# Second cross-attention of a perceiver block: probabilities turned in 32x32 blocks on VectorE, weighted means in four row tiles of TensorE, key rows fetched ready from DRAM

## The reference

```python
xn = layer_norm(x, g_media, b_media)          # x: context, 64 x 257 x 128
ln = layer_norm(latents, g_latent, b_latent)  # 64 x 32 x 128
q = (ln @ Wq).reshape(B, Q, 16, 64).transpose(0, 2, 1, 3) * scale
kv = jnp.concatenate([xn, ln], axis=1) @ Wkv
k, v = jnp.split(kv, 2, axis=-1)              # each 16 heads of 64
sim = jnp.einsum('bhqd,bhfd->bhqf', q, k)
sim = jnp.where(full_mask[:, None, None, :], max_neg, sim)   # latents are never masked
alphas = jax.nn.softmax(sim, axis=-1)
out = jnp.einsum('bhqf,bhfv->bhqv', alphas, v)
return out.transpose(0, 2, 1, 3).reshape(B, Q, 1024) @ Wout + bout
```

## Time and profile before

| | us |
|---|---|
| median of 3 runs | 1558.25 |
| lowest and highest of them | 1556.33, 1567.27 |
| the profiled execution, its time | 1562.48 |
| the profiled execution, span from first to last instruction | 1560.7 |
| experts, from the first to the last of their `up` products | 464 to 700 |
| second cross-attention, its scores from first to last | 760.4 to 1307.9 |
| second cross-attention, last product | 1317 |

### The profile page before, as it was taken

The page is one execution under the profiler, slowest core; times in us unless marked ns, Lnnn a source line. Parts: engine busy times, 40 slices in busy tenths (PEclk is TensorE's granted clock), DMA queues, the critical chain, the costliest instruction groups (busy, mean ns, idle before and its releaser), DMA issues. The chain is left out here.

```text
span 1560.7 us, 36610 instructions
## 1 busy us (share of the span) xinstructions
PE 1362.0 (87%) x12406; PEld 1038.3 (67%) x12406; DVE 851.6 (55%) x2728; ACT 804.3 (52%) x1838; POOL 146.0 (9%) x432
## 2 busy tenths in 40 slices
PE   5799999666759999997899999999999999577855
PEld 2677777366536777775688888888888887212433
DVE  3466666478433444444555555555555554654387
ACT  3588888278314444442555555455555554444423
POOL 0122221364001111110000000000000000000000
PEclk8899999899669999997999999999999999787965
DMA  3332331000012111110000000000000000000000
GB/s 96 89 75 73 76 74 50 1 0 0 0 52 86 55 55 47 48 41 0 20 17 16 21 15 19 15 19 15 19 15 19 15 21 4 1 0 1 20 1 27
DMA packets 58225, 47.58 MB, mean 30 GB/s; under 512 B 11048, under 2 KB 55600, under 8 KB 58032
## 3 DMA queue, kind: packets, MB, share of 16 engines
q1 hardware_dynamic: 58160, 46.74, 10.9%
HBM read 36.07 MB, written 1.18 MB: 24 GB/s over the span
## 5 line engine op out<-in xcount | busy, mean ns | idle before, releaser
L1426 ACT ACTIVATE d_p<-bank,d_nmax 128x289 f32<-128x289 f32 x256 | 128.8, 503 | 239.0 <-DVE d_nmax L1472 238.9
L1364 PE MATMUL bank<-d_pT,d_xv 128*128 128x128 f32 x1536 | 220.3, 280 | 0.1
L1472 DVE TENSOR_REDUCE d_nmax<-bank 128x1 f32<-128x289 f32 x256 | 116.7, 456 | 171.3 <-PE bank L1345 169.6
L1364 PEld LDWEIGHTS bank<-d_pT,d_xv 128*128 128x128 f32 x1536 | 191.3, 191 | 12.1 <-ACT d_pT L1418 6.3
L1344 PE MATMUL bank<-d_key,d_q 128*128 128x289 f32 x512 | 167.3, 408 | 0.6 <-ACT d_q L1411 0.4
L1162 ACT ACTIVATE c_hs<-bank,c_w 128x512 f32<-128x512 f32 x128 | 87.8, 687 | 147.1 <-PE bank L1085 145.6
L431 ACT ACTIVATE a_p<-a_p,a_nmax 128x257 f32<-128x257 f32 x256 | 115.5, 500 | 38.6 <-DVE a_nmax L470 38.5
L1353 PE MATMUL bank<-ident,d_p 128*128 128x128 f32 x768 | 125.9, 273 | 0.1
L1418 ACT ACTIVATE d_pT<-bank 128x384 f32<-128x384 f32 x256 | 123.0, 480 | 0.9 <-PE bank L1353 0.8
L1085 PE MATMUL bank<-yT,c_w 128*128 128x512 f32 x256 | 118.2, 606 | 6.0 <-DMA c_w<-in_L_ffn_w 6.0
L1094 PE MATMUL bank<-c_w,c_hs 128*128 128x128 f32 x1024 | 122.0, 278 | 0.0
(11 more groups left out here) (268 smaller groups left out, 2304.6 us busy)
## 6 DMA issues: line engine op xcount, KB each, us to landing
d_key<-x_keyT SPq DMA_DIRECT2D x64, 144.5 KB
a_ctT<-in_ctxT SPq DMA_DIRECT2D x64, 128.5 KB, 2.1
a_low<-mask_low SPq DMA_DIRECT2D x64, 128.5 KB, 3.0
c_ct<-in_ctx SPq DMA_DIRECT2D x64, 128.0 KB, 2.2
c_w<-in_L_ffn_w SPq DMA_DIRECT2D x8, 514.0 KB, 3.8
xT<-in_xT SPq DMA_DIRECT2D x4, 256.0 KB, 3.5
a_vlast<-values_last SPq DMA_DIRECT2D x4, 256.0 KB, 6.4
d_maskb<-mask_bf SPq DMA_DIRECT2D x64, 0.5 KB
```

Source lines behind the costliest of these rows:

```text
L1364: ins = nc.tensor.matmul(OP[:, 128 * g:128 * g + 128], xv[:, b % 2, k, :], pT[:, u % 2, k, :], start=(k == 0), stop=(k == 2))
L1426: nc.scalar.activation(P[:, u % 4, 0:KEYS], S[u % 2], ACT.Exp, bias=nmax[:, u % 4:u % 4 + 1], accum_out=total[:, u % 4:u % 4 + 1]).then_in ...
L1472: nc.vector.tensor_reduce(nmax[:, u % 4:u % 4 + 1], S[u % 2], AXX, ALU.max, negate=True).then_inc(max_made, 1)
```

## The change

1. In the experts, VectorE now applies the whole affine layer norm to the context rows: `normalise` has two passes over the four tiles, `(x - mean) * gamma` and then `* rstd + beta`, each a `scalar_tensor_tensor` with a row of `x_media` (gamma and beta along the free axis, the same in all partitions). A new semaphore `centred` stands between them. `keep` becomes a plain copy, with the keys in another order.
2. SyncE stores each pair's finished rows to a DRAM tensor `key_rows` (64 batches x 32 x 10 x 128): key 8k+r of a batch lies at [k][r], row 8 of each k holds a latent, row 9 the last context row or zeros. The store of a pair is four transfers of 64 KB, issued ahead of the load of a later pair.
3. The mask is stored as float32 `-3.39e38` times the mask, in the new key order, and is fetched for each batch to all 128 partitions (`d_low`).
4. In the cross-attention TensorE no longer adds the mask, transposes the probabilities or makes key rows. Scores read `keyT` directly. The custom instruction adds the mask, writes the scores to SBUF and gives the maximum; ScalarE's exponential runs in place there; GpSimd normalises; VectorE turns the probabilities in 32x32 blocks into `d_pT`. Key k of block r then lies on partition k of each row tile, where row tile j holds head j of each group.
5. `means` is, once for a batch, ten blocks x four row tiles of 32 partitions: 40 products, each 32 keys by 128 columns, tile j into bank 2+j. The key rows come from DRAM, 32 partitions x 5120 bytes repeated four times in one transfer (`d_xr`, two slots).
6. Queries and projection are spread out: four products of each in every batch. ScalarE copies the means out. The final normalisation writes over `yT`.

```diff
@@ class Context
+        self.media, self.blank = sb("x_media", [128, 2, 128]), sb("x_blank", [128, 128])
+        self.low_dram = core.nc.dram_tensor("mask1_low", (BATCH, CTX + LAT), F32, kind="Internal").ap()
+        self.rows_dram = core.nc.dram_tensor("key_rows", (BATCH, 32, 10, 128), F32, kind="Internal").ap()
...
@@ experts_0, sync
+                def store_pair(i, s):
+                    sp.wait_ge(normed, i * UNITS + (s + 2))
+                    for b in range(2):
+                        for k in range(2):
+                            rows = cx.rows_dram[bass.ds(i * (2 * UNITS) + (2 * s + b), 1), 16 * k:16 * k + 16, 0:8, :].rearrange("b k r d -> (b k) r d")
+                            sp.dma_start(rows, ct[:, s % RING, 2 * b + k, :]).then_inc(cx.rows_stored[s % RING], 16)
+
+                def next_pair(i, s):
+
+                    store_pair(i, s - 3)
+                    sp.wait_ge(turned, i * UNITS + (s - RING + 2))
+                    sp.wait_ge(cx.rows_stored[s % RING], (i * 2 + s // RING) * 64)
+                    load_pair(i, s)
...
@@ experts_0, scalar, keep
-                        keys = cx.keyT[:, bass.ds(i * (2 * UNITS) + 2 * s, 2), 0:256]
-                        src = TC[s % 2].rearrange("p (b k) -> p b k", b=2)
-                    nc.scalar.activation(keys, src, ACT.Identity, scale=cx.affine[:, 0:1], bias=cx.affine[:, 1:2]).then_inc(kept, 1)
+                        keys = cx.keyT[:, bass.ds(i * (2 * UNITS) + 2 * s, 2), 0:256].rearrange("p b (r k) -> p b k r", r=8)
+                        src = TC[s % 2].rearrange("p (b k r) -> p b k r", b=2, r=8)
+                    nc.scalar.activation(keys, src, ACT.Copy).then_inc(kept, 1)
...
@@ experts_0, vector, normalise
                     for m in range(tiles):
-                        ins = nc.vector.tensor_scalar(ct[0:rows, at, m, :], ct[0:rows, at, m, :], moments[0:rows, at, m, 0:1],
-                                                      rstd[0:rows, at, m:m + 1], ALU.subtract, ALU.mult)
+                        ins = nc.vector.scalar_tensor_tensor(ct[0:rows, at, m, :], ct[0:rows, at, m, :], moments[0:rows, at, m, 0:1],
+                                                             cx.media[0:rows, 0, :], ALU.subtract, ALU.mult)
+                    ins.then_inc(centred, 1)
+                    dve.wait_ge(centred, i * UNITS + (s + 2))
+                    for m in range(tiles):
+                        ins = nc.vector.scalar_tensor_tensor(ct[0:rows, at, m, :], ct[0:rows, at, m, :], rstd[0:rows, at, m:m + 1],
+                                                             cx.media[0:rows, 1, :], ALU.mult, ALU.add)
                     ins.then_inc(normed, 1)
...
@@ cross_attention_1, sync
+                def rows(i, b, first=False):
+
+                    n = i * EIGHT + b
+                    if not first:
+                        sp.wait_ge(o_made, n - 1)
+                    rows = cx.rows_dram[bass.ds(n, 1)].rearrange("b k r d -> b k (r d)").broadcast_to([4, 32, BLOCKS * 128])
+                    sp.dma_start(xr[:, b % 2].rearrange("p r d -> p (r d)"), rows).then_inc(xr_loaded[b % 2], 16)
...
@@ cross_attention_1, gpsimd
+                def normalise(i, u):
+                    b, g = divmod(u, GROUPS)
+                    pool.wait_ge(recip, i * UNITS + (u + 1))
+                    p = P[:, b % 2, g, 0:KEYS]
+                    nc.gpsimd.tensor_tensor(p, p, rtotal[:, b % 2, g:g + 1].broadcast_to([128, KEYS]), ALU.mult).then_inc(normed, 1)
...
@@ cross_attention_1, tensor
+                def means(i, b, first=False):
+
+                    n = i * EIGHT + b
+                    pe.wait_ge(xr_loaded[b % 2], (i * (EIGHT // 2) + b // 2) * 16 + 16)
+                    pe.wait_ge(turned, (n + 1) * GROUPS)
+                    if not first:
+                        pe.wait_ge(o_copied, n)
+                    for k in range(BLOCKS):
+                        for j in range(4):
+                            rows = slice(32 * j, 32 * j + 32)
+                            ins = nc.tensor.matmul(O[j], xr[rows, b % 2, k, :], pT[rows, b % 2, :, 32 * k:32 * k + 32], start=(k == 0), stop=(k == BLOCKS - 1))
+                    ins.then_inc(o_made, 1)
...
@@ cross_attention_1, vector
+                    dve.wait_ge(s_made, i * UNITS + (u + 1))
+                    nc.vector.nop(nofuse=True)
+                    nc.vector.tensor_tensor_reduce(P[:, b % 2, g, 0:KEYS], S[u % 2], low[:, b % 4, :], -1.0, 3.4e38, ALU.add, ALU.min,
+                                                   accum_out=nmax[:, b % 2, g:g + 1]).then_inc(max_made, 1)
...
+                    dve.wait_ge(normed, i * UNITS + (u + 1))
+                    if g == 0 and not (first and b < 2):
+                        dve.wait_ge(o_made, i * EIGHT + (b - 1))
+                    nc.vector.transpose(pT[:, b % 2, g, :], P[:, b % 2, g, :]).then_inc(turned, 1)
```

More of the change, by code:

```diff
@@ L17 @@
 EPS = 1e-5
+LOWEST = -3.3895313892515355e38
 class Core:
@@ L1299, in _ @@
+                for b in range(EIGHT):
+                    if b >= 4:
+                        mask(0, b)
+                    rows(0, b, b < 2)
                 with sp.Fori(1, TURNS) as i:
-                    for b in range(8):
-                        load(i, b)
+                    for b in range(EIGHT):
+                        mask(i, b)
+                        rows(i, b)
             @block.gpsimd
             def _(pool):
-                nc.gpsimd.memset(lowest[:], 0.0).then_inc(low_made, 1)
@@ L1324, in queries @@
-                def queries(i, g, r, first=False):
-                    if not (first and r < 2):
-                        pe.wait_ge(q_copied, (i * 2 + g) * 4 + (r - 1))
-                    if r == 0 and not first and not (isinstance(i, int) and i * 2 + g < 2):
-                        pe.wait_ge(out_added, i * 2 + (g - 1))
+                def queries(i, b):
+                    r, ahead = b % 4, b // 4 + 1
+                    if not (isinstance(i, int) and (i * 2 + ahead) * 4 + r == 0):
+                        pe.wait_ge(q_copied, (i * 2 + ahead) * 4 + r)
@@ L1382, in body, with scores @@
[L1382 to L1395 removed]
+                def scores(i, b, g, first):
+                    u = b * GROUPS + g
+                    if g == 0 and b % 4 == 0:
+                        pe.wait_ge(q_copied, (i * 2 + b // 4) * 4 + 4)
+                    if not (first and u < 2):
+                        pe.wait_ge(max_made, i * UNITS + (u - 1))
+                    nc.tensor.matmul(S[u % 2], q[:, b // 4, b % 4, 4 * g:4 * g + 4, :].rearrange("p h q -> p (h q)"),
+                                     keyT[:, bass.ds(i * EIGHT + b, 1), :].rearrange("p a k -> p (a k)"), start=True, stop=True).then_inc(s_made, 1)
@@ new lines, in project @@
+                def project(i, b):
+                    ago, r = divmod(b - 5, 4)
+                    if r == 0:
+                        pe.wait_ge(o_copied, (i * 2 + ago + 1) * 4)
+                        if not (isinstance(i, int) and i * 2 + ago == 0):
+                            pe.wait_ge(out_added, i * 2 + ago)
+                    for h in range(4 * r, 4 * r + 4):
+                        ins = nc.tensor.matmul(OUT, wvo[:, h, :], a[:, ago % 2, h].rearrange("p b q -> p (b q)"), start=(h == 0), stop=(h == HEADS - 1))
+                    if r == 3:
+                        ins.then_inc(out_made, 1)
@@ new lines, in body @@
+                def body(i, first, last):
+                    for b in range(EIGHT):
+                        scores(i, b, 0, first)
+                        scores(i, b, 1, first)
+                        if not (last and b >= 4):
+                            queries(i, b)
+                        scores(i, b, 2, first)
+                        scores(i, b, 3, first)
+                        if not (first and b < 5):
+                            project(i, b)
+                        if not (first and b == 0):
+                            means(i, b - 1, first and b == 1)
@@ L1397, in _ @@
+                for m in range(TILES):
+                    ins = nc.tensor.transpose(core.bank[:, 2 + m // 4, 128 * (m % 4):128 * (m % 4) + 128], latT[:, 128 * m:128 * m + 128], core.ident[:])
+                    if m % 4 == 3:
+                        ins.then_inc(lat_turned, 1)
+                for r in range(4):
+                    queries(-1, 4 + r)
+                pe.wait_ge(latents_placed, 1)
+                pe.wait_ge(lat_kept, NCH)
                 peeled(pe, TURNS, body)
-                transposes(TURNS, -2)
@@ new lines, in exponential, with means @@
+                def exponential(i, u):
+                    b, g = divmod(u, GROUPS)
+                    act.wait_ge(max_made, i * UNITS + (u + 1))
+                    p = P[:, b % 2, g, 0:KEYS]
+                    nc.scalar.activation(p, p, ACT.Exp, bias=nmax[:, b % 2, g:g + 1], scale=-1.0,
+                                         accum_out=total[:, b % 2, g:g + 1]).then_inc(exp_made, 1)
```

(16 more changed lines are left out.)

291 lines of the change are left out of this document (113 added, 178 removed).

## The result

| | before | after |
|---|---|---|
| median, us | 1561.71 (4 runs) | 1710.29 (4 runs) |
| lowest and highest | 1556.33, 1567.27 | 1702.40, 1717.82 |
| profiled execution: time, span | 1562.48, 1560.7 | 1702.40, 1700.5 |

The changed kernel is **slower**: the ratio is 1.0946, with a 95% interval of 1.0907 to 1.0984. The forecast was 1466 with a range of 1435 to 1530. It missed by 244 us, and on the other side of no change.

What follows compares the result with a forecast made beforehand. The prediction took TensorE's instruction list and waits to bound both stages. Cross-attention -133, experts' second pass +37 and stage ends +4 gave -92 us, taking the median from 1558.25 to 1466, range 1435 to 1530.

Steps and rivals of the forecast that it cites:

- Transfers ... Cost 0: Cross-attention fetch on SyncE: 640 KB of key rows land in about 4.8 us, needed 10 us after issue; cost 0.
- transfers late: Rival: transfers come late, at 1 us for each us of delay and batch; some 1500 to 1560 us, chance 0.04.
- still a unit ahead: Experts, SyncE: each pair's load, behind four stores, is issued a unit before its statistics; cost 0, bounds 0 and 10 us.
- a batch of 6.5 us: Cross-attention: TensorE's work takes 6.5 us a batch after the change, against 8.59 before; -133 us over 63.75 batches.
- the second pass of +37: Experts: VectorE's added normalising pass delays all 32 sets by 1.17 us each; +37 us, bounds 25 and 50.
- the row tiles' loads are hidden: Cross-attention means: weight loads overlap streaming in row tiles, so a round of four costs 0.111 us.
- 2.23 + 0.43: Cross-attention means, per batch: 20 rounds of four products take 2.23 us, and changing the array's tiling twice takes 0.43.
- Loads not hidden: Rival, cross-attention means: load and stream alternate in each row tile, 0.22 us a round; 1606 us, slower, chance 0.09.
- tiles in series: Rival, cross-attention means: row tiles run one after another, 8.9 us for 80 instructions; 1893 us, chance 0.03.
- a partly hidden second pass: Rival, experts: part of VectorE's second normalising pass is hidden; 1430 to 1440 us, chance 0.04.
- shut out by GpSimd: Rival, cross-attention: VectorE's block transposition waits up to 0.9 us for GpSimd's multiplication; 1517 to 1568 us, chance 0.10.
- The factor 3.07: Skill's gain for four row tiles, set against the forecast: a batch would cost 7.2 us, the time about 1511.

## Why the prediction was wrong

- **The step that failed is "Transfers ... Cost 0".** It took the landing of 640 KB in proportion to the 514 KB of `c_w` in 3.8 us, 4.8 us. But `c_w` has 128 rows as its outermost dimension, and in the changed kernel's trace it keeps 0.73 of the 16 engines busy, at 255 GB/s (611 to 612); the key rows have four entries, keep 0.27 busy and move 84. The rate was carried over from a transfer of another form, and the packets alone take 6.3 us. The step also priced the key rows by themselves: it gave the mask, queued behind them, no landing time, and it took 11.2 us. Of the 181 us, some 129 came by that way. The batches became 2.8 us longer (9.61 against 6.80 in the mean).
- **The rival "transfers late" named the place but not the price.** It stood at 1500 to 1560 with a chance of 0.04, without a mechanism. The shape `[4, 32, 1280]`, set beside that of `c_w`, would have given it one.
- **In the experts the store's price was looked for at the pair's load**, "still a unit ahead". Behind that load stands the expert's weight load, which the step did not follow: it went out 11.1 us later in its unit, with 9.3 us of lead before. The measured price is 35 us instead of 0, outside the bounds of 0 and 10.
- **A term was missing**: the return of TensorE's loop, 32 us. The cross-attention's rows of before could not show it, since the old loop, also of eight batches, has no such wait; its body has some 134 matmuls and weight loads a batch by the prediction's own list, the new one 208.
- **The sum of the work was right to within 4 us.** With these three terms taken off, 1710.3 - 181.3 - 35.0 - 31.9 = 1462 us, where the forecast said 1466. Its stated bounds, 1440 to 1495, are narrower than its own terms give (1435 to 1506), and nothing turned on that. Point by point: a batch of 6.5 us came out at 6.34; the second pass of +37 at 38.7 with what the latents' rows cost taken in; the row tiles' loads are hidden. In the run with the loop written out, the starts of the 20 rounds of four are 0.112 us apart but for the first step of 0.213, and from the first to the next other instruction it is 2.44 us, so that with the gap of 0.2 in front the means take about what was forecast (2.23 + 0.43). Loads not hidden, tiles in series and a partly hidden second pass all fell.
- **VectorE was not shut out by GpSimd.** The transposition's row, beside GpSimd's 0.67 us in every unit:

```profile
L1505 DVE STREAM_TRANSPOSE d_pT<-d_p x256: 490/494/515, 834.1 to 1442.7; 128x320 f32<-128x320 f32 x128
```

254 of the 256 transpositions overlap in time with a multiplication of GpSimd, and none takes more than 515 ns. That it has one SBUF input was the reason given; the rows bear out the result, and no run here varied the inputs.
- The factor 3.07 of the Trainium skill (TensorE: Matmul & The Clock Gate, Part 3) would have made the batch 7.2. The same 80 instructions at 0.111 in the full array would be 8.9 us, so 2.44 is a gain of 3.6. The page's factor is for 512 columns; for float32 tiles of 128 columns this case comes out above it. The case also disagrees with the page's statement that loads overlap only across row groups: each round's loads go to the tiles that are streaming, and the rounds are 0.112 us apart, as in the full array.

## What to carry to other kernels

Before a landing time is carried from one transfer to another, compare their outermost dimensions, not only their bytes: a broadcast written as a leading dimension of four cut the engines from 16 to 4, and four plain transfers of the same bytes gave 181 us back. When stores are put into an in-order queue, follow every issue behind them up to the one that is needed soonest, and ask what the stores wait for, not only how long they take to issue. And when a change is large and the time moves the wrong way, its parts can all be right: here the kernel came out some 140 us faster than before, once the fetch, the weights' place and the loop were mended and the second pass, 39 us, was taken out again.

## What the runs showed of the hardware

- A packet of 5120 B took 196 ns in the median of the stages in which key rows ran on four engines or on two, and 323 ns in the stretch with all 16 busy. Four engines moved 84 GB/s and 16 moved 253: an engine moves less when all run, but all together three times as much.
- A transfer of 16 engines behind one of four in the same queue is held back in part: of the mask's 128 packets 96 started about 1 us after the issue, the last 32 of the one issued at 1008.35 after 8.4 to 10.8 us, and it took 11.2 us to land instead of 3.2.
- At each of five returns of TensorE's loop of eight batches (some 1660 matmuls and weight loads) TensorE stood about 3.7 us without a semaphore to wait for, and then ran at half its clock. Nine instruction packets of 16 KB were fetched in each turn, and TensorE went on 1.8 to 2.2 us after the second one at the return had ended. The loop before, of some 1070, fetched none in the same stretch and showed no such wait. That the row tiles use instructions up fast (80 products and 80 loads in 2.5 us) does not decide it: written out, the same list ran at the same pace without a wait. Between which lengths of body the change lies is not shown, as only these two were run.
